# Group 1's layer norm moved into the turned layout, with its mean and deviation brought back from memory as rows, in a fused layer norm and graph network kernel on one Trainium2 core

## What is computed

```python
h = jnp.maximum(_layernorm(x, axis=-1), 0.0)      # (x - mean) / sqrt(var + 1e-5), over features
# gnn(h, adj):
#   x_conv = relu(bn2(conv17(relu(bn1(conv1(h))))) + h)      conv along the nodes
#   s = h @ w_se.T + b_se;  A = exp(-|s_n - s_m|^2) * adj
#   x_nmp = A @ relu(h @ w_msg.T + b_msg)
#   r, z, n: GRU gates from [x_conv, x_nmp] and h
#   result = (1 - z) * tanh(gi_n + r * gh_n) + z * h
x = x + gnn(h, adj)
```

## Time and profile before

| | us |
|---|---|
| median of 3 runs | 289.75 |
| lowest and highest | 289.58, 289.75 |
| profiled execution, its own time | 289.65 |
| span of its profile | 287.5 |
| TensorE busy in the span | 276.3 (96%) |
| VectorE busy in the span | 249.8 (87%) |

### The profile page before, as it was taken

One profiled execution on the slowest core, in us unless ns is written; L12 is line 12 of the kernel. 1 busy time (PEld: TensorE's weight loads), 2 busy tenths in 40 slices (PEclk: granted clock), 3 DMA queues, 4 the chain that ended last, 5 costly groups with the idle time before them and its releaser, 6 DMA issues.

```text
span 287.5 us, 5282 instructions
## 1 busy us (share of the span) xinstructions
PE 276.3 (96%) x1866; PEld 248.8 (87%) x1866; DVE 249.8 (87%) x565; ACT 164.5 (57%) x271; POOL 49.7 (17%) x110
## 2 busy tenths in 40 slices
PE   7799899999998999999999999999999999999993
PEld 5498886998887998899888998899988998899993
DVE  6998988988998889978998889979898887986565
ACT  3785468745665267555675266563674366561363
POOL 7400020810015002320025002230025000130000
PEclk9999999999999999999999999999999999999998
DMA  7900014534241402532041312523012120001002
GB/s 240 372 22 0 6 70 146 138 135 169 75 148 38 163 23 74 185 105 81 21 195 43 116 69 74 183 72 114 2 67 117 39 74 2 29 7 39 0 2 73
DMA packets 9437, 25.36 MB, mean 88 GB/s; under 512 B 2626, under 2 KB 3140, under 8 KB 8644
## 3 DMA queue, kind: packets, MB, share of 16 engines
q1 hardware_dynamic: 9264, 25.03, 25.0%
q10 hardware_dynamic: 148, 0.01, 0.0%
HBM read 20.79 MB, written 4.24 MB: 87 GB/s over the span
## 4 chain that ended last, share of the span: by engine, by line
PE 67%; DVE 17%; issue 7%; ACT 5%; POOL 2%; DMA 1%; DVEq 0%; ACTq 0%; POOLq 0%
PE ps L1190 20%; PE ps L1192 19%; PE ps L1191 19%; PE ps L1274 4%; PE ps L1240 3%; DVE stats L747 2%; DVE wt_lo L789 2%; ACT wt_hi L448 1%; POOL rstd L376 1%; PE ps L1251 1%; DMA xin<-x_first 1%; DVE aff L945 1%; DVE v_lo L870 1%; DVE y L890 1%; PE ps L1264 1%
## 5 line engine op out<-in xcount | busy, mean ns | idle before, releaser
L1190 PE MATMUL ps<-v_hi,wt_hi 128*128 128x256 f32 x320 | 92.6, 289 | 3.1 <-DVE y L909 1.5
L1192 PE MATMUL ps<-v_hi,wt_lo 128*128 128x256 f32 x320 | 90.1, 282 | 0.0
L1191 PE MATMUL ps<-v_lo,wt_hi 128*128 128x256 f32 x320 | 89.9, 281 | 0.0
L1190 PEld LDWEIGHTS ps<-v_hi,wt_hi 128*128 128x128 f32 x320 | 60.3, 188 | 5.1 <-DVE wt_lo L789 1.8
L1191 PEld LDWEIGHTS ps<-v_lo,wt_hi 128*128 128x128 f32 x320 | 60.3, 188 | 0.3
L1192 PEld LDWEIGHTS ps<-v_hi,wt_lo 128*128 128x128 f32 x320 | 60.2, 188 | 0.0
L382 POOL TENSOR_TENSOR scale<-vpe,neg_half 128x8 f32<-128x8 f32 x6 | 10.6, 1767 | 110.5 <-DVE scale L764 110.5
L1190 PE MATMUL ps<-h_hi,wt_hi 128*128 128x512 f32 (+1 forms) x67 | 26.3, 392 | 0.3 <-DVE h_lo L799 0.2
L1192 PE MATMUL ps<-h_hi,wt_lo 128*128 128x512 f32 (+1 forms) x67 | 25.8, 386 | 0.0
L1191 PE MATMUL ps<-h_lo,wt_hi 128*128 128x512 f32 (+1 forms) x67 | 25.7, 384 | 0.0
L600 ACT ACTIVATE gate<-ps,par 128x512 f32<-128x512 f32 x14 | 9.6, 687 | 20.6 <-PE ps L1192 20.6
(11 more groups left out here) (160 smaller groups left out, 613.2 us busy)
## 6 DMA issues: line engine op xcount, KB each, us to landing
w<-ln_rows SPq DMA_DIRECT2D x6, 1024.0 KB, 4.7
mask<-adj_t SPq DMA_DIRECT2D x8, 512.0 KB, 3.4
xt<-x_t SPq DMA_DIRECT2D x8, 512.0 KB, 3.3
out<-gate SPq DMA_DIRECT2D x15, 256.0 KB, 2.0
xin<-x_nm SPq DMA_DIRECT2D x6, 512.0 KB, 3.3
w<-w_conv SPq DMA_DIRECT2D x1, 576.0 KB, 6.4
gate<-w_gate SPq DMA_DIRECT2D x1, 576.0 KB, 7.4
xin<-x_first SPq DMA_DIRECT2D x2, 256.0 KB, 2.9
```

What stands on the lines that cost most here:

```text
L1190: pe.matmul(dst, wt_hi[:, blk, :], hi, start=start, stop=False)
L1191: pe.matmul(dst, wt_hi[:, blk, :], lo, start=False, stop=False)
L1192: return pe.matmul(dst, wt_lo[:, blk, :], hi, start=False, stop=stop)
```

## The change

Group 1 is treated as groups 2 to 7 are. Its x comes as `x_nm` for the statistics; `moments(1)` stands right behind `ln_stats(1)` in VectorE's order, ahead of `masked(0,0)`; `ln_scale(1)` takes the place of the third step of `ln_scale_first`; SyncE gets `column_rows(1)` behind the load of the second mask; `ln_apply(1,0)` and `ln_apply(1,1)` stand on VectorE where the four normalisations stood, ahead of `reset(0,0)`; ScalarE gets `h_high(1,0)` and `h_high(1,1)` between `reset_rows(0,0)` and `update_rows(0,0)`, and `graphs_of(1,c)` around `candidate(0,0)`. The eight transposes of group 1 and the waits before them are gone, as are the eight normalisations, the two `h_rows` and the two `by_graphs` of group 1. The load of the next `xin` and of `xts[2]` are issued behind `column_rows(1)`.

The core of the diff (the renumbering of semaphore counts for all groups is left out):

```diff
@@ sync @@
-                sp.wait_ge(wt_lo_ready, LOT_OF_GATES)
-                if g > 2:
+                sp.wait_ge(wt_lo_ready, LOT_OF_SUB[8])
+                if g > 1:
                     sp.wait_ge(hf_ready, NCH * g)
...
-            sp.dma_start(xin[:], x_first[1]).then_inc(x_landed, 16)
+            sp.dma_start(xin[:], x_nm[0]).then_inc(x_landed, 16)
...
             sp.wait_ge(a_ready, NCH)
             sp.dma_start(mask[:], adj_t[1]).then_inc(mask_landed, 16)
-
-            sp.wait_ge(hn_ready, 2 * NCH)
-            sp.wait_ge(hn_first, 3)
-            sp.dma_start(xin[:], x_nm[0]).then_inc(x_landed, 16)
-
-            sp.wait_ge(ht_ps, 2 * NCH)
+            column_rows(1)
+            sp.wait_ge(stats_ready, 2)
+            sp.dma_start(xin[:], x_nm[1]).then_inc(x_landed, 16)
+
+            sp.wait_ge(ht_ps, NCH)
             sp.dma_start(xts[2][:], x_t[2]).then_inc(xt_landed[2], 16)
@@ gpsimd @@
-            ln_scale_first(2)
-            pool.wait_ge(rstd_first, 3)
+            ln_scale(1)
+            pool.wait_ge(scale_ready, 1)
@@ scalar @@
             reset_rows(0, 0)
-            ln_rows_first(1)
+            h_high(1, 0)
+            h_high(1, 1)
             update_rows(0, 0)
+            graphs_of(1, 0)
             candidate(0, 0)
-            h_rows(1, 0, 0)
-            h_rows(1, 1, 1)
-            by_graphs(1, 0, 0)
-            by_graphs(1, 1, 1)
+            graphs_of(1, 1)
             conv1_rows(1, 0, 2)
@@ vector @@
             ln_stats(1)
+            moments(1)
             masked(0, 0)
             masked(0, 1)
...
             join_y(0, 1, 1)
-            dve.wait_ge(stats_ready, 2)
-
-            dve.wait_ge(hn_ready, NCH)
-            some_moments(slice(0, GB))
-            ln_first(2, slice(0, GB))
             xc_low(0, 0)
             xc_low(0, 1)
-            dve.wait_ge(rstd_first, 3)
-            offset(slice(4, GB))
-
-            dve.wait_ge(ht_ps, NCH)
-            hn_rows_first(slice(0, 4))
+            ln_apply(1, 0)
+            ln_apply(1, 1)
+            h_low(1, 0)
             reset(0, 0)
+            h_low(1, 1)
             update(0, 0)
-            h_low(1, 0)
-            h_low(1, 1)
             ln_stats(2)
@@ tensor @@
             gates_h(0, 1, True)
-            h_transpose(1, 0, 0)
-            h_transpose(1, 1, 1)
             gates_n(0, 1)
```

More of the change, by code:

```diff
@@ L284, in _ @@
         def _(sp):
-            sp.dma_start(xin[:, 0:4, :], x_first[0, :, 0:4, :]).then_inc(xh_landed, 16)
-            sp.dma_start(xin[:, 4:8, :], x_first[0, :, 4:8, :]).then_inc(x_landed, 16)
+            sp.dma_start(xin[:, 0:4, :], x_first[:, 0:4, :]).then_inc(xh_landed, 16)
+            sp.dma_start(xin[:, 4:8, :], x_first[:, 4:8, :]).then_inc(x_landed, 16)
             sp.dma_start(w_a[:], w_in).then_inc(wa_landed, 16)
@@ L294, in column_rows @@
             def column_rows(g):
-                sp.wait_ge(scale_ready, g - 1)
-                upto(sp, col_landed, 16 * (g - 2))
+                sp.wait_ge(scale_ready, g)
+                upto(sp, col_landed, 16 * (g - 1))
                 sp.dma_start(ln_rows.rearrange("k (p b) -> p k b", b=GB), scale[:]).then_inc(rows_stored, 16)
-                sp.wait_ge(rows_stored, 16 * (g - 1))
-                sp.wait_ge(wt_lo_ready, LOT_OF_GATES)
-                if g > 2:
+                sp.wait_ge(rows_stored, 16 * g)
+                sp.wait_ge(wt_lo_ready, LOT_OF_SUB[8])
+                if g > 1:
                     sp.wait_ge(hf_ready, NCH * g)
@@ L315, in _ @@
             sp.dma_start(mask[:], adj_t[1]).then_inc(mask_landed, 16)
-            sp.wait_ge(hn_ready, 2 * NCH)
-            sp.wait_ge(hn_first, 3)
-            sp.dma_start(xin[:], x_nm[0]).then_inc(x_landed, 16)
-            sp.wait_ge(ht_ps, 2 * NCH)
+            column_rows(1)
+            sp.wait_ge(stats_ready, 2)
+            sp.dma_start(xin[:], x_nm[1]).then_inc(x_landed, 16)
+            sp.wait_ge(ht_ps, NCH)
             sp.dma_start(xts[2][:], x_t[2]).then_inc(xt_landed[2], 16)
             sp.wait_ge(stats_ready, 3)
-            sp.dma_start(xin[:], x_nm[1]).then_inc(x_landed, 16)
+            sp.dma_start(xin[:], x_nm[2]).then_inc(x_landed, 16)
             column_rows(2)
@@ L339, in _ @@
                     sp.wait_ge(stats_ready, g + 3)
-                    sp.dma_start(xin[:], x_nm[g + 1]).then_inc(x_landed, 16)
+                    sp.dma_start(xin[:], x_nm[g + 2]).then_inc(x_landed, 16)
                 if g + 2 < NG:
@@ L368, in ln_scale_first @@
             def ln_scale_first(step):
-                tiles = (slice(0, 4), slice(4, GB), slice(0, GB))[step]
+                tiles = (slice(0, 4), slice(4, GB))[step]
                 pool.wait_ge(vpe_first, step + 1)
-                if step == 2:
-                    pool.wait_ge(hn_ready, NCH)
-                    pool.wait_ge(hn_first, 2)
                 pool.tensor_tensor(rstd[:, tiles], vpe[:, tiles], neg_half[:, tiles], ALU.pow).then_inc(rstd_first, 1)
             def ln_scale(g):
-                pool.wait_ge(vpe_ready, 2 * (g - 1))
-                upto(pool, rows_stored, 16 * (g - 2))
+                pool.wait_ge(vpe_ready, 2 * g)
+                upto(pool, rows_stored, 16 * (g - 1))
                 pool.tensor_tensor(scale[:, 1, :], vpe[:], neg_half[:], ALU.pow).then_inc(scale_ready, 1)
@@ L422, in _ @@
                     ln_scale(g + 1)
-                    pool.wait_ge(scale_ready, g)
+                    pool.wait_ge(scale_ready, g + 1)
                 distances(pool, g)
@@ L448, in lot_high, with ln_rows_first @@
                 act.activation(wt_hi[:, first:first + count, :], source, ACT.Copy).then_inc(wt_hi_ready, 1)
[L450 to L455, removed]
+            def ln_rows_first():
+                act.wait_ge(rstd_ready, 1)
+                for j in range(6, GB):
                     last = act.activation(hn[:, j, :], xin[:, j, :], ACT.Identity, bias=nmr[:, j:j + 1],
@@ L469, in hf_rows_first, with by_graphs_first @@
                     act.activation(hf[0][:, cols(c)], bank(src), ACT.Relu).then_inc(hf_ready, 1)
-            def by_graphs(g, c, src):
-                upto(act, msg_ps, g)
+            def by_graphs_first(c, src):
                 act.activation(hg[:, :, c * HALF:(c + 1) * HALF], bank(src).rearrange("p (n b) -> p b n", b=GB),
@@ L488, in graphs_of @@
                                ACT.Copy).then_inc(hg_ready, 1)
[L490 to L496, removed]
             def conv1_rows(g, c, src):
@@ L642, in _ @@
             lot_high(0)
-            ln_rows_first(0)
+            ln_rows_first()
             h_rows_first()
@@ L656, in _ @@
             lot_high(4)
-            by_graphs(0, 0, 6)
-            by_graphs(0, 1, 3)
+            by_graphs_first(0, 6)
+            by_graphs_first(1, 3)
             lot_high(5)
@@ L750, in moments @@
                 dve.wait_ge(stats_ready, g + 1)
-                dve.wait_ge(hn_ready, 2 * NCH)
-                dve.wait_ge(hn_first, 3)
-                upto(dve, vpe_ready, 2 * (g - 2))
+                dve.wait_ge(hn_ready, NCH)
+                dve.wait_ge(hn_first, 2)
+                upto(dve, vpe_ready, 2 * (g - 1))
                 for j in range(GB):
@@ L757, in moments @@
                 last.then_inc(mv_ready, 1)
-                dve.wait_ge(mv_ready, g - 1)
-                dve.wait_ge(rstd_first, 3)
-                upto(dve, scale_ready, g - 2)
+                dve.wait_ge(mv_ready, g)
+                dve.wait_ge(rstd_first, 2)
+                upto(dve, scale_ready, g - 1)
                 dve.tensor_scalar(vpe[:], mv[:, :, 1], EPS, None, ALU.add).then_inc(vpe_ready, 1)
-                upto(dve, rows_stored, 16 * (g - 2))
+                upto(dve, rows_stored, 16 * (g - 1))
                 dve.tensor_copy(scale[:, 0, :], mv[:, :, 0]).then_inc(vpe_ready, 1)
             def ln_apply(g, c):
-                dve.wait_ge(col_landed, 16 * (g - 1))
+                dve.wait_ge(col_landed, 16 * g)
                 dve.wait_ge(xt_landed[g % 3], 16 * (g // 3 + 1))
-                dve.wait_ge(diff_ready, NCH * (g - 2) + c + 1)
+                upto(dve, diff_ready, NCH * (g - 2) + c + 1)
                 dst = hf[g % 2][:, cols(c)]
@@ L774, in ln_apply @@
                                   ALU.subtract).then_inc(centred, 1)
-                dve.wait_ge(centred, NCH * (g - 2) + c + 1)
+                dve.wait_ge(centred, NCH * (g - 1) + c + 1)
                 dve.scalar_tensor_tensor(out=dst, in0=dst, scalar=0.0, in1=col_ln[:, 1, cols(c)], op0=ALU.max,
@@ L792, in h_low @@
             def h_low(g, c):
[L793 to L796, removed]
+                dve.wait_ge(h_hi_ready, NCH * (g - 1) + c + 1)
                 upto(dve, z_ps, NCH * (g - 2) + c + 1)
@@ L1192, in three, with h_transpose @@
                 return pe.matmul(dst, wt_lo[:, blk, :], hi, start=False, stop=stop)
[L1194 to L1208, removed]
+            def h_transpose(c, dst):
+                pe.wait_ge(hn_first, c + 1)
+                if c:
```

(9 more changed lines are left out.)

1 line of the change is left out of this document (removed).

## The result

The changed kernel takes 294.76 us (median of 6 runs, 294.16 to 295.66) against 289.58 for the kernel before (6 runs, 289.56 to 289.75): a ratio of 1.0182, 95% interval 1.0164 to 1.0200. It is slower by 5.2 us, by the forecast's sign and inside its range, 0.7 above the predicted 294.1. Its profiled execution took 294.74 us, with a span of 292.9.

A forecast was written before the change was run, and what follows sets the result against it. Two chains, VectorE's and TensorE's, were taken to bound the edited stretch, the later setting the rest. Profiled 289.65 plus TensorE's 4.5 (3.3 and 1.2 for the clock) less a tenth gave 294.05, as median 294.1 us; range 291.9 to 295.9.

The forecast's parts named there:

- Moments earlier: VectorE before masked(0,0): 2.50 us in place of 1.55, so masked(0,0) and all that hangs on it come 0.95 us later.
- When the rows land: SyncE's queue: store issued at 36.21, down at 39.2 just after the mask, load of rows 5.0 us more.
- T: The moment when group 1's rows have landed and ln_apply(1,0) can start; forecast 44.2, bounds 42.5 and 44.5.
- VectorE's chain from T: From ln_apply(1,0) through update(0,0): ln_stats(2) starts at T + 8.24, a VectorE delay of 3.9 us.
- T - 40.27: VectorE's delay at ln_stats(2) against the kernel before, 3.9 us at T = 44.2.
- TensorE's chain from T: z gate of gates_h(0,1) starts at T + 4.02, a new 3.5 us wait; TensorE's delay 3.3 us without the clock.
- T - 40.88: TensorE's delay after subtracting 0.79 for removed transposes and the 0.18 wait before conv1(1,0): 3.3 us.
- The clock in the sum: TensorE's clock falls in its wait, costing 1.2 us; with 3.3 that makes 4.5, the later chain.
- rival B: Rows are late but the clock holds; VectorE's chain sets the end, 293.6 us; chance 0.28.
- Rival C: Store does not stay behind the mask: T = 42.5 to 43.1, no fall of the clock, 292.2 us; chance 0.17.
- Rival D: Rows are there before VectorE asks: T = 41.4, delay 1.1, 290.8 us; chance 0.05.
- Rival E: TensorE alone sets the end; removed transposes and two waits gain 1.1 us, 288.6 us; chance 0.03 for faster.

The follow-up runs named there:

- before_mom: The kernel before the change, with only group 1's moments moved up between ln_stats(1) and masked(0,0): 290.21 us, ratio 1.0021.
- rows_first: The changed kernel with column_rows(1), the store, put ahead of the load of the second mask on SyncE: 293.90 us, ratio to before 1.0146.
- clock_kept: The changed kernel with 16 idle matmuls on TensorE in its wait before the z gate of gates_h(0,1): 294.86 us, ratio to before 1.0178.
- gates_first: The changed kernel with group 0's reset and update ahead of ln_apply(1,0) on VectorE, update_rows and candidate ahead of h_high on ScalarE: 295.16 us.
- pe_extra: The kernel before the change, with four idle matmuls added on TensorE behind group 1's eight transposes: 289.70 us, ratio 1.0002.
- rows_reset: The changed kernel with rows_first's store order, reset(0,0) ahead of ln_apply(1,0), both h_low ahead of update(0,0), and gates_first's ScalarE order: 292.07 us.
- warm_near: rows_first with one more 4 KB store issued near 33.5 us and a wait until it landed: 293.38 us (2 runs).

## Why the prediction came out as it did

**Moments earlier: right in size, its reach read short.** 2.50 us from the statistics to `masked` came out exactly, as did the wait of 0.94 at `gather(0,0)` and the mask's issue at 35.56 net. That TensorE's lateness also reaches VectorE's chain was seen only in before_mom, where it costs 0.6 us. In the changed kernel it lies under the wait for the rows.

**When the rows land: the store was mis-sized.** Forecast: issued 36.21, down 39.2, rows after 5.0 more, T = 44.2. Net: issued 36.47, as GpSimd's power took 1.97 us where it took 1.69 for group 2 before; down 40.57; rows after 4.5; T = 45.12. The step "So I take 39.2, just after the mask" is the one that failed: I had the mask landed at 38.96 and the store on its heels; the mask landed at 39.06 and the store was down 1.4 us later than I had it. rows_first shows 1.5 us of the mask's doing and 1.0 that even an empty queue doesn't remove.

**VectorE's chain from T: right.** T + 8.24 for `ln_stats(2)`; it was T + 8.20. The formula T - 40.27 gives 4.85 with the true T. The kernel's profiled execution is 5.09 us longer, 4.78 without the 0.31 of the first load.

**TensorE's chain from T: near, by two errors that cancel, and not in charge.** T + 4.02 for the z gate; it was T + 4.03. At `messages(1)` TensorE was 5.58 - 0.31 = 5.27 us late, where T - 40.88 and 1.2 for the clock make 5.44. Both terms were too small in size. From the z gate to `messages(1)` it is 5.95 us before, 6.00 after, and 4.62 in clock_kept: the slow clock cost 1.4, not 1.2, and the missing transposes and the wait before `conv1(1,0)` gave back 1.3, not 0.79 + 0.18.

**The clock in the sum: wrong.** "TensorE's delay is then 3.3 + 1.2 = 4.5 us, the later chain" failed on the slack. I gave `sub_conv(1,3)` a tenth of a microsecond between bank and start. Its distance from the four matmuls before it is 0.73 us before (59.33 to 60.06) and 0.36 after (64.91 to 65.27), so before the change TensorE had some 0.4 us of wait at that bank that the rows didn't label as one. Its delay shrinks there from 5.58 to 5.21, and the tenth by which that is over VectorE's 5.11 goes in the wait for VectorE's y at 69.73, which the prediction didn't count. clock_kept settles it: 1.3 us of TensorE's time back, none of the kernel's. So the predicted 294.1 was near by luck: the clock's 0.6 stood in for the 0.9 by which T was too early. What happened is rival B with a later T, although the clock did fall. The range's upper end doesn't follow from its terms either: T = 44.6 and 2.1 for the clock make 295.5, not 295.9. That this slack is thin shows in gates_first, where VectorE was 2 us earlier and the slow clock did cost. The changed kernel's runs vary by 1.5 us, with mean clocks from 0.994 in the fastest to 0.988 in the two slowest; that its slower runs are those in which TensorE's chain overtakes is likely but argued from these means only, and clock_kept, at 294.74 to 295.15, has no run as fast as its fastest.

**Rival C** (the store does not stay behind the mask) is out: with the mask moved away the store is 1.5 us faster. **Rival D** is out: VectorE waited 3.68 us for the rows. **Rival E** is out: pe_extra shows that TensorE's time at the transposes was worth nothing, so that its removal could not pay.

**Where the 5.2 us are.** 2.4 is what rows_reset keeps with no wait for the rows. Its rows on VectorE account for it: from `reset(0,0)` on, the four `ln_apply` add 2.65 us, the two `h_low` take 1.39 in place of 1.21, and the wait of 0.79 for the tanh is filled, together 2.0; `ln_stats(2)` is 2.0 late. The 1.1 us of normalisations that went pay nothing there, as VectorE waits for `reset_rows(0,0)` in their place, which TensorE's lateness from `gather(0,0)` on delays. The remaining 2.7 is the wait for the rows and the order of work: 0.9 for the queue behind the mask (rows_first) and 1.8 for the order, with the clock's fall that goes with it (rows_reset against rows_first). The 0.6 of before_mom is not a share beside these: the wait for the tanh through which it came is absent in rows_reset. The shares are differences between medians, good to a few tenths.

**Open:** why this one store takes 2.6 to 3.1 us in every version with an empty queue, when the later ones take 1.6. In rows_first one packet of another queue, which the profile calls instruction, moved in the same microsecond:

```profile
q1 hardware_dynamic: 234, 0.01, 12.7%
q8 instruction: 1, 0.02, 5.8%
```

The traces show more than this coincidence. A packet of that queue lies in the flight of group 1's store in all ten traces that have this store, and in none of the 78 stores of 1.6 us in the thirteen traces. And of the 272 packets of the store, all move between 0.8 and 1.2 us after the issue in a store of 1.6 us (52.97 before); in rows_first and rows_reset 255 do, and the last 17, a sixteenth, come at 1.4 to 2.0. With 16 DMA engines on a core this looks like the share of one engine that the instruction packet held up, but the trace doesn't name the engine, no version moved that packet, and the slow stores are reported 0.8 us or more after their last packet, where it is 0.4 in the fast one. So the cause is not shown.

## What to carry to other kernels

A round trip through memory is priced from the moment its store can be issued to the moment its load has landed, here 8.6 us for 8 KB out and 1 MB back, and whatever stands in the same queue just ahead belongs to it. Before a step is taken off the busiest engine, add work to that engine at the same place: if this costs nothing, as four matmuls did here, its removal will pay nothing either. That holds for this place alone: the same engine 0.9 us late ten microseconds earlier, at `gather(0,0)`, cost 0.6. When a wait can't be avoided, put the work that doesn't need the data ahead of it on every engine in the chain, ScalarE's order too: together with the store ahead of the mask that returned 2.7 of the 5.2 us here (0.9 for the store's place, 1.8 for the order), but not the 2.4 that the additional VectorE work costs.

## What the runs showed of the hardware

TensorE's clock fell in a wait of 4.5 us (after). With waits of 2.9, 3.1 and 3.3 us (warm_near, rows_first, gates_first) it fell only after the work had resumed: in gates_first the first four matmuls behind the wait still start 0.34 and 0.23 us apart, and only from 52.15 on 0.43. 16 idle matmuls in the wait kept it at 2.4 GHz (clock_kept). GpSimd's power on 128 x 8 took 1.97 us after a wait of 24 us and 1.72 for group 2's, after a wait of 20 us; why is open.
